# A two-layer decoder on one core: the causal maximum's scores of four heads issued together every second round

## The reference

```python
dot_scores = jnp.einsum('bhtd,bhsd->bhts', q3, k3) * scale
geo_bias = q_on_dir[..., :, None] * k_on_dir[..., None, :]
scores = jnp.where(causal, dot_scores + geo_bias, -jnp.inf)
attn = jax.nn.softmax(scores, axis=-1)
out = jnp.einsum('bhts,bhsd->bhtd', attn, v)
```

## Time and profile before

| | |
|---|---|
| median of 3 runs | 1193.17 us (1192.88 to 1196.08) |
| the profiled execution | 1193.53 us |
| its span, first to last instruction | 1191.8 us |
| TensorE matrix products busy | 1089.6 us, 91% of the span |
| the same between 24 and 190 us, where the changed products stand | 154.5 of 166.0 us, granted clock 0.93 |

### The profile page before, as it was taken

How to read it: one execution, slowest core, us unless ns; L and a number is a source line. 1 busy time by engine, 2 the same in 40 slices (tenths; PEclk the granted TensorE clock), 3 DMA queues, 4 the chain that set the end, 5 groups by cost and what they waited for, 6 DMA issues and landing times.

```text
span 1191.8 us, 19630 instructions
## 1 busy us (share of the span) xinstructions
PE 1089.6 (91%) x7306; PEld 689.9 (58%) x7306; DVE 744.2 (62%) x1092; ACT 550.5 (46%) x1044; POOL 111.3 (9%) x133
## 2 busy tenths in 40 slices
PE   5999989888788988789889999999999999999997
PEld 3443443432222322368666777877778787788664
DVE  3432555589999998553336566466666776776257
ACT  2434335155455556722126566356644554466320
POOL 2001123020200000010000000010002000120020
PEclk9999889799899999899999999999999999999999
DMA  5614003210000000000035333114432633220001
GB/s 153 170 71 150 10 22 112 91 65 14 14 14 14 15 1 1 1 19 1 1 72 147 72 72 72 37 45 99 107 72 54 153 88 76 68 72 1 1 1 36
DMA packets 56493, 67.89 MB, mean 57 GB/s; under 512 B 14665, under 2 KB 35922, under 8 KB 56402
## 3 DMA queue, kind: packets, MB, share of 16 engines
q1 hardware_dynamic: 55234, 65.06, 20.9%
q10 hardware_dynamic: 1168, 1.57, 0.4%
HBM read 30.96 MB, written 13.63 MB: 37 GB/s over the span
## 4 chain that ended last, share of the span: by engine, by line
PE 74%; DVE 13%; issue 5%; ACT 4%; DMA 1%; SPq 1%; ACTq 0%; POOL 0%; DVEq 0%; POOLq 0%
PE p_ring L1725 11%; PE p_unit L1725 11%; PE p_out L1872 10%; PE p_ring L1769 9%; PE p_ring L1849 9%; PE p_ring L1746 6%; PE p_out L1838 5%; PE p_ring L1815 5%; DVE halves L1496 4%; DVE prob_a L1510 2%; PE p_ring L1793 2%; DVE x L1695 2%; PE p_unit L1950 2%; ACT prob_b L1296 1%; PE p_unit L1904 1%
## 5 line engine op out<-in xcount | busy, mean ns | idle before, releaser
L1310 ACT ACTIVATE prob_a<-p_ring 128x1024 f32<-128x1024 f32 x128 | 130.5, 1022 | 97.4 <-PE p_ring L1815 97.1
L1475 DVE TENSOR_REDUCE nmax<-p_ring 128x2 f32<-128x1024 f32 (+1 forms) x128 | 156.0, 1219 | 30.1 <-PE p_ring L1769 30.1
L1496 DVE TENSOR_REDUCE halves<-p_ring 128x2 f32<-128x1024 f32 x128 | 155.8, 1220 | 27.5 <-PE p_ring L1793 27.1
L1296 ACT ACTIVATE prob_b<-p_ring,nmax 128x512 f32<-128x512 f32 (+1 forms) x192 | 158.6, 837 | 30.9 <-DVE nmax L1475 30.7
L1328 ACT ACTIVATE probT_b<-p_ring 128x512 f32<-128x512 f32 x144 | 84.5, 598 | 189.5 <-PE p_ring L1849 187.9
L1769 PE MATMUL p_ring<-stacks 128*128 128x512 f32 x512 | 150.8, 417 | 9.2 <-ACT prob_b L1296 5.4
L1529 DVE COPY probT_b<-p_ring 128x512 f32<-128x512 f32 x112 | 77.1, 688 | 114.6 <-PE p_ring L1849 114.3
L1849 PE MATMUL p_ring<-ident,prob_b 128*128 128x128 f32 x1024 | 134.6, 274 | 0.3 <-ACT probT_b L1328 0.3
L1849 PEld LDWEIGHTS p_ring<-ident,prob_b 128*128 128x128 f32 x1024 | 116.2, 141 | 23.6 <-issue 15.2
L1815 PE MATMUL p_ring<-x_q,x_kq 32*128 32x512 f32 x512 | 119.4, 648 | 2.3 <-DVE halves L1496 2.1
L1769 PEld LDWEIGHTS p_ring<-stacks 128*128 128x128 f32 x512 | 86.9, 189 | 26.2 <-ACT prob_b L1296 10.0
(11 more groups left out here) (208 smaller groups left out, 1537.9 us busy)
## 6 DMA issues: line engine op xcount, KB each, us to landing
stacks<-splitH_b SPq DMA_DIRECT2D x80, 128.0 KB, 2.3
stacks<-splitL_b SPq DMA_DIRECT2D x80, 128.0 KB, 2.4
stacks<-x_kd SPq DMA_DIRECT2D x32, 256.0 KB, 4.6
x_kd<-early SPq DMA_DIRECT2D x8, 512.0 KB, 3.8
x_v<-x_vd SPq DMA_DIRECT2D x8, 512.0 KB, 4.1
x_vd<-early SPq DMA_DIRECT2D x6, 512.0 KB, 2.8
a_st<-a_image SPq DMA_DIRECT2D x32, 64.0 KB, 2.7
x_kd<-xT SPq DMA_DIRECT2D x4, 512.0 KB, 3.1
```

Source lines behind the costliest of these rows:

```text
L1296: ins = nc.scalar.activation(prob_b[:, n % NP_SLOTS, a * 512:a * 512 + w_all], p_scores[:, n % 2, a * 512:a * 512 + w_all], ACT.Exp, bias= ...
L1310: nc.scalar.activation(prob_place(key), slot_of("S2", key), ACT.Exp, accum_out=x0_sums[:, m:m + 1]).then_inc(done["E2"], 1)
L1475: nc.vector.tensor_reduce(nmax[:, n % 4, 0:heads], src, AX.X, ALU.max, negate=True).then_inc(done["M"], 1)
L1496: nc.vector.tensor_reduce(to, src, AX.X, ALU.max, negate=True).then_inc(done["M1"], 1)
```

## The change

In `paired_stream` a round that takes an A0 `S1` item now takes the next one, pr 1, as well (`its`), and the round after takes none (`resting`). Both `S1` steps are added one behind the other, then both `M1` steps. On TensorE, an item with pr 0 issues its two score products and no mask; the item with pr 1 issues its own two, then the two mask products of pr 0 with the semaphore increment of pr 0, then its own two with its increment. X0's `S1` items stay one a round. The number and form of all products stay as they were, the list has the same number of rounds (477), and the places in the ring are dealt in the new order.

```diff
+    resting = False
...
-        if f < len(first) and may_score(first[f]):
-            it = first[f]
-            f += 1
+        its = []
+        if f < len(first) and resting:
+            resting = False
+        elif f < len(first) and may_score(first[f]):
+            its = first[f:f + 2] if first[f][0] == "A0" else first[f:f + 1]
+            resting = len(its) == 2
+        f += len(its)
+        for it in its:
             sched.add("S1", *it)
+        for it in its:
             sched.add("M1", *it)
...
+                        if pr == 0:
+                            continue
+                        first_pair = (*key[:5], 0)
+                        for aa in range(2):
+                            ins = nc.tensor.matmul(slot_of("S1", first_pair)[:, aa, w - 128:w], identb[:, :], hidden[:, :],
+                                                   start=False, stop=True)
+                        ins.then_inc(done["S1"], 1)
                         for aa in range(2):
                             ins = nc.tensor.matmul(o[:, aa, w - 128:w], identb[:, :], hidden[:, :], start=False, stop=True)
```

## The result

| | before | after |
|---|---|---|
| median | 1195.3 us (5 runs beside it, 1192.88 to 1196.08) | 1217.3 us (5 runs, 1214.24 to 1221.35) |
| ratio | | 1.0195, 95% interval 1.0175 to 1.0214 |
| profiled execution, span | 1193.53, 1191.8 us | 1216.56, 1214.8 us |
| mean granted clock of the span | 0.973 | 0.963 |

The changed kernel is slower by 22 us, 23.0 in span. The forecast was 13.7 more, 1206.9, with a range that ended at 1216: the sign was right and the size too small. Three executions in a slow state (two of the kernel before at 1585.9 and 2596.8 us, one of experiment e2 at 1246.5) are left out of every number here.

A forecast was written before the change was run, and what follows sets the result against it. TensorE's own work was taken as the bound, busy 154.5 of 166 us from 24 to 190 us. Net waits by stretch summed to 13.7 us: 1193.53 + 13.7 - 0.36 = 1206.9 us, range 1195 to 1216.

The forecast's parts named there:

- the sign: Whole kernel: slower, because ring waits outweigh the cheaper pairs; slower in all had chance 0.76.
- A: Double units, 68.0 to about 103 us: second S1 of a pair waits for drains and exponentials, +2.8 us.
- C: Two x_v units, then dt and rb, from 137.0 us: waits for drains, E2 and two maxima, +1.9 us.
- B: No units, 119.81 us to mt at 129.17: waits for E2 and M1, +1.6 us with what stands behind.
- the start: Start of A0: second kd waits for its drain, mt for two maxima, part regained while values are projected, +1.3 us.
- 103 to 118.8: Stretch behind the double units, walked in the prediction as 103 to 120.8 us: +0.5 us.
- from there to X0's first exponential: Group from 152 to 169 us +2.0, group to 192 us +2.6, last six S2 of A0 +1.0 us.
- rival 3: Between 24 and 190 us: more waits bring more half-clock stretches, 1211 to 1217 us, chance 0.12.
- The saving of 7.7 us of work: 32 pairs of A0 on TensorE: 29.5 us before, 21.8 us after, if TensorE never waited.
- t + 0.33: TensorE's cost of a pair in us, instead of 2 (t + 0.21); t from 0.26 to 0.44, on average 0.35.
- waits of 13.7 + 7.7 = 21.4 us: Added waits at A0's ring: net 13.7 us, with the cheaper pairs' 7.7 us already taken off.
- 1 and 2: First: waits hidden, faster, 1185.5 us, chance 0.11. Second: waits fill only what cheaper pairs free, 1193 us, chance 0.13.

The follow-up runs named there:

- e2: Changed kernel with the two S1 ahead of the S2 in a round, in X0 too: 1231.7 us, ratio 1.034.
- e5: Kernel before with DVE's maxima and ACT's exponentials in A0 cut to 64 columns a head: 1178.9 us.
- e10: Kernel before with pr 1 taken first where an S2 of pr 0 stands ahead of a query tile's first S1: 1193.3 us, ratio 1.0001.
- e15: Kernel before with each query tile's first S1 on other rows than the S2 ahead, and A0's mt one round later: 1193.3 us, ratio 0.9988.
- e9: Kernel before with each maximum of A0 taken twice on DVE, TensorE's order and work unchanged: 1218.9 us.
- e13: Changed kernel with unit mt of each A0 group placed one round later: 1206.1 us.
- e14: Changed kernel with unit mt placed one round later for the first A0 group alone: 1212.2 us.
- e1: Changed kernel's order of steps, but each S1 issues its own two mask products as in the kernel before: 1229.1 us.
- e6: Changed kernel with DVE's maxima and ACT's exponentials in A0 cut to 64 columns a head: 1195.3 us.
- e12: Changed kernel with only ACT's exponentials in A0 cut to 64 columns a head: 1206.0 us.

## Why the prediction was right or wrong

**The sign, and who waits: right.** TensorE's idle time from 24 to 204 us grew to 180.0 - 154.6 = 25.4 us (promised: more than 25). L1790 waits 10.5 us there, 6.6 of it for ACT's and DVE's readings and drains (2.6 before) and 3.9 for loads. That is less than the prediction put there: more of the new idle time stands ahead of the units, 4.8 us at `mt` (1.3 before) and 3.3 at `rb` (0.5 before). The maxima come in twos. Most of the delay is there by the end of A0, and nothing takes it back: X0 starts 21.7 us late and ends 20.4 late (first and last exponential), so it is as long as before, as promised. What stands behind it takes 702.3 us against 699.7. A0's last `S1` starts 15.6 us later (forecast 12).

**The walks along the order: right at A and C, for B in the sum alone, wrong at the start.** Counted from the start of each place, in the changed kernel's profile:

| place | forecast | measured |
|---|---|---|
| start, to 68.0 | +1.3 | +6.6 |
| A, double units | +2.8 | +3.1 |
| 103 to 118.8 | +0.5 | +0.4 |
| 118.8 to 137.0 (B and what follows) | +1.6 | +0.7 |
| C, to unit rb | +1.9 | +1.9 |
| from there to X0's first exponential | +5.6 | +9.0 |

Their sum is 21.7 us, the delay of X0. In A the walk from 68.0 had the second item of the first pair 1.4 us in, that of the second 10.3 and of the third 16.0; they stand at 1.39, 10.48 and 16.36 behind 74.59. In C it had rb at 10.9; it stands at 158.91 - 147.8 = 11.1. In B it had `mt` wait 1.0 us behind two maxima. That `mt` (129.17 before, 142.25 after) doesn't wait; the one ahead of it (118.77 before, 128.87 after) waits 1.64 us, and from one to the other takes 3.0 us longer, all of it at half clock, of which 2.3 come back by the end of the row. One thing was not forecast: at 108.65 the scores waited 0.59 us for a load, which I had costed at nothing.

**The step that failed: the granted clock.** The sum was made at the clock of the kernel before, and the clock was put aside as rival 3 with 0.12. It is a term of the sum. The earlier trace rows already had it: 0.93 in A0, with two half-clock stretches. If waits cost clock there, the waits that I added had to cost some too. Without the clock the split gives 15.1 - 3.1 = 12.0 us up to X0, near the forecast's 13.7, and the runs at one clock +15.2. The clock adds 9.6 in the profile, and 0.0095 x 0.77 / 0.001 = 7.3 us in the timed runs. Of the 9.6, the start holds 6.7: a half-clock stretch of 6.8 us before, two of 13.7 and 10.2 us after. Its +6.6 are +6.7 of clock, +3.1 of idle time and -3.2 of work. Not all of that is the change's: e5, e10 and e15, in the old order, have one stretch of 10.2 us there. The prediction's own check (clock of A0 under 0.90) came out at 0.86. Its price in rival 3, 3.5 to 10 us, was the right one; the chance was not.

e9 shows the link between waits and clock without the change, with the one doubt named there. e13 shows that a wait taken away by order alone gives time back, but not that the clock rises with it. It was only argued, and e13 and e14 speak against it, that this or that wait brings this or that stretch.

The Trainium skill ("TensorE: Matmul & The Clock Gate", section "A second HAM failure mode: psum-queue depth-cycling") describes a kernel whose TensorE idles in small pieces as it goes round its PSUM places and whose clock goes up and down between the two levels for it. This case agrees: three places in the ring, waits of mostly 0.3 to 1.7 us, and 61 instead of 38 us at 1.2 GHz. By that rule rival 3 would have been the forecast.

**Two terms with errors that offset each other.** The saving of 7.7 us of work was 3.1. A pair costs t + 0.33 only if both items' places are free and no `S2` runs on the rows of one of them. All four started together in 11 of 32 pairs, 5 of them in the start, where no `S2` runs yet, and there the work falls by 3.2 us; behind it nothing is saved. In 8 pairs I had charged the wait of the second item and kept the gain that this wait destroys. The other way, waits of 13.7 + 7.7 = 21.4 us were in the sum, and 15.1 more of idle time came. What I counted as waits at the second item is probably in part time in which both had to run anyway. That the two errors nearly cancel, so that 12.0 us without the clock stand beside a forecast of 13.7, is luck.

**Rivals.** 1 and 2 needed the ring's waits to be rare or to fall under other work; TensorE idled ahead of the second item in 8 of 32 pairs and ahead of `mt` and `rb`, 15.1 us more in all. Rival 3 gave 1211 to 1217 us, and 1217.3 came.

## What to carry to other kernels

Work it out at a place, not by the sum: a pair that shares an engine only shares it when both of its buffers are free and nothing else holds the rows of one of them, and here a ring of three places and the `S2` ahead took that away in most pairs. Where the granted clock stands under 1 in the stretch that a change touches, put the clock into the sum: here it added some 0.6 us to each us of new idle time. When two changes of order are compared, compare them at one clock too, since here it moved one and the same kernel by some 12 us.

## What the runs showed of the hardware that I had not expected

The mean granted clock of one and the same kernel ranged from 0.964 to 0.980 and its time from 1189.9 to 1202.9 us. In e5, shorter readings by DVE and ACT left TensorE's work and nearly all its idle time as they were and took the time lost to the clock from 17.9 to 6.2 us; the idle time as a sum is thus not what decides it. In e1 less idle time went with more lost clock (a mean clock of 0.956 against 0.963).

Scores on free rows seem to start ahead of scores that stand before them in the list: at 190.98 us of the changed kernel an `S2` starts on the rows of pr 0; two of the pair's scores start at 190.99 and the other two at 191.32, though the pair's first item is pr 0. That the early two are pr 1 is read from their offsets and durations alone.

What decides the clock is open: no run here holds TensorE's instructions and waits fixed and changes the rest alone. In e5 (and e6 and e12) the products of `PV` also read exponentials that were not renewed, and no run tells whether that plays a part.
